# Two row blocks of attention joined behind the experts, with the last chunk settled inside, and a shorter lag

## The chip, the cores and the metric

One NeuronCore of a Trainium2 chip runs the whole program. The metric is the device time of one execution in microseconds. The median of three runs of the kernel before is 915.72 us.

## The reference

Input: `x` (64, 64, 64, 4) and `txt` (64, 32, 64), float32; 64 batches, T = 96 tokens (64 made from `x`, 32 from `txt`), width 64.

```
h = concat(mean over hidden of (x @ W^T + b), txt)      # (64, 96, 64)
h = h + state_space_layers(layernorm(h))                # four layers
h = h + moe(layernorm(h))                               # 16 experts, top 2, then a layernorm
h = h + attention(layernorm(h))                         # 8 heads of width 64
h = h + recurrence(layernorm(h))                        # 96 steps over the tokens

attention: q, k, v = x Wq + bq, ...;  scores = q k^T / 8
           position i sees j < i only; row 0 is all zero;  out = softmax(scores) v Wu + bu
recurrence: i, g, o from xt U + b + h V;  c' = h c + i g;  h' = o tanh(c')
```

Since a token sees only earlier ones, attention can be done in blocks of 32 rows (tokens), each of which needs only the tokens up to its end, and the recurrence can run as soon as the row block of its step is done.

## The kernel before

All work is one program over five engines that hand over by semaphores. What follows the state-space layers is a sequence of NSLOT = 152 slots (the loops `for g in range(NSLOT)` of GpSimd, ScalarE, VectorE and TensorE). NPR = 96 of them are expert slots: in each, TensorE does one pair of experts for 512 tokens, `up` (L1491, 4 matmuls) and `down` (L1478) of two slots ago, VectorE weighs the input (`weigh`, L1004), ScalarE applies the relu (L684, or L686 and L688 in halves). Eight slots finish a quarter-chunk product that ScalarE copies out (`product_out`, L675). Sixteen slots finish a chunk of 16 tokens; there are NC = 6 chunks, two to a row block.

A finished chunk is *settled* in parts at slots given by SB and LATER (LAST for the last chunk): `sums_out` turns the sums through PSUM bank 7 (L1393), VectorE adds them (`settle` 0 to 3), centres them, GpSimd squares them (L547), takes the power -1/2 (L550), multiplies (L553) and applies gamma (L557), twice (second time for the attention's norm), `norm_out` turns the result (L1400), and two copies on ScalarE (`turned`, L670) and two on VectorE (parts 13, 14, L996) put it where attention reads it. `borrow` makes TensorE wait until the last reader has freed bank 7.

AT names the slots after which the slot loop stops and a row block of attention is done: 47, 79 and 107. Row block 0 has 4 units, block 1 has 8, block 2 has 16; a unit is (row block, group of 16 batches, share of the group), and a group makes one unit in block 0, two in block 1, four in block 2. (The prediction calls them the first, second and third attention, or row blocks 1, 2 and 3 as the change's title does.) For a group TensorE makes *queries* in two halves into banks 6 and 7 (L1504); ScalarE copies bank 6 (`u_out`, L694) and VectorE bank 7 (L1015). For a unit: scores (L1518, or L1525 with the mask L1528); in block 0 the mask is added by VectorE (L1048) and the scores are turned (`turn_s`, L1536); VectorE takes the maximum (L1054) and subtracts it (L1058); ScalarE exponentiates (L715); VectorE sums (L1036) and inverts (L1039 to L1043); GpSimd multiplies (L581); TensorE turns the probabilities (`turn_p`, L1546) and the keys (`turn_keys`, L1556); ScalarE copies the first (L729), VectorE the second (L1066); `gather` (L1574) multiplies them, its results are copied by both engines (L706, L1027); `project` (L1585) closes a group and ScalarE copies the output with the bias (L720).

Inside an attention all engines walk x over the units and a tail. In round x the unit x is scored, x - 2 is turned, x - 3 gathered, x - 4 projected (DRAIN = 4). On ScalarE, the exponential of unit x comes first in the round, then the copies of the next group's queries; `next_u` says in which round a group's two query halves are made. Attention starts only when all four engines have finished their slots, and TensorE waits for all of its copies before it goes on.

The recurrence: step t runs in slot LS0 + t = 56 + t (`step_at`): TensorE `gates_h` (L1454, 12 matmuls of 32 columns), ScalarE tanh of the gates (L743; from step 52 on L745 and L747), VectorE L1107 and L1113, ScalarE L751, VectorE L1120 and L1122; every four steps `gates_x` makes the next inputs (L1440) and `out_tp` turns outputs (L1469). So 24 steps share slots 56 to 79 with experts, 16 share 80 to 95, 12 run in 96 to 107 beside the last chunk's settling, and 44 run alone. Before the steps of a chunk, the attention output of that chunk must be turned (`att_out`, L1409), added, normalised and copied (`att_residual`, `norm`, `normed`, `turn_x`, `copy_x`, L737): the parts of XLATER at the slots of XB.

## Time and profile before

| | us |
|---|---|
| median of 3 runs | 915.72 |
| lowest and highest | 906.75, 916.69 |
| the profiled execution | 910.88 |
| its span | 909.2 |
| TensorE, VectorE, ScalarE, GpSimd busy | 714.3, 556.1, 344.6, 251.5 |
| mean granted TensorE clock | 0.827 of full |

All stretches below are cut from this one execution; the time of an execution is its span and 1.7 us around it. A busy share over the whole span says little here, because stages with different limits follow one another.

### The profile page before, as it was taken

The numbers are of one execution on the slowest core, as the hardware profiler recorded it, in microseconds if no ns is written. First come the engines' busy times: TensorE is split into PE (matmuls) and PEld (weight loads), VectorE is DVE, ScalarE is ACT, GpSimd is POOL, SyncE is SP. The second block draws the span as 40 slices with busy tenths as digits, with TensorE's granted clock in tenths as the row PEclk, the third lists the DMA queues.
The fourth block names the chain that finished last, engine by engine and source line by source line (L and its number), as shares of the span: only waits on it lengthen the run. The fifth ranks groups of instructions, "written<-read, shape, count | busy, mean of one in ns | idle before, by whom it ended". The sixth has DMA issues, their size and how long they took to land.

```text
span 909.2 us, 16503 instructions
## 1 busy us (share of the span) xinstructions
PE 714.3 (79%) x6414; PEld 420.1 (46%) x6414; DVE 556.1 (61%) x1128; ACT 344.6 (38%) x656; POOL 251.5 (28%) x223
## 2 busy tenths in 40 slices
PE   4686888654799998567899987978985599976675
PEld 3673656344322222254234435654434377755554
DVE  4848557769566563552685757657846477746543
ACT  2232343424244554123435543354442244432332
POOL 3338567547000330100240212212313032311100
PEclk9998887965599999668999998899975599985555
DMA  9730000000253341000222200002200000000000
GB/s 189 122 70 4 2 1 1 1 1 0 82 168 115 107 141 32 1 1 1 93 76 77 94 36 1 1 9 75 59 4 7 6 2 1 2 1 6 8 9 13
DMA packets 42403, 36.86 MB, mean 41 GB/s; under 512 B 20888, under 2 KB 29848, under 8 KB 42328
## 3 DMA queue, kind: packets, MB, share of 16 engines
q1 hardware_dynamic: 41242, 35.57, 14.9%
q8 instruction: 52, 0.85, 0.4%
q10 hardware_dynamic: 1088, 0.26, 0.2%
q14 instruction: 21, 0.17, 0.1%
HBM read 33.85 MB, written 1.97 MB: 39 GB/s over the span
## 4 chain that ended last, share of the span: by engine, by line
PE 51%; DVE 28%; ACT 8%; issue 6%; POOL 2%; DMA 2%; SPq 1%; POOLq 0%; DVEq 0%; ACTq 0%
PE PS L1491 9%; PE PS L1478 9%; PE PS L1454 4%; PE PS L1504 3%; PE PS L1525 3%; PE PS L1574 3%; PE PS L1585 2%; DVE XC L863 2%; PE PS L1546 2%; DVE am L1054 2%; DVE LS L1113 2%; DVE st L845 2%; DMA BIG<-in_x 2%; PE PS L1556 2%; ACT Y L639 2%
## 5 line engine op out<-in xcount | busy, mean ns | idle before, releaser
L1491 PE MATMUL PS<-Y,W1f 64*128 64x512 f32 x384 | 114.4, 675 | 4.5 <-DVE Y L1004 2.9
L1478 PE MATMUL PS<-XC,w2s 128*64 128x512 f32 x384 | 106.4, 635 | 0.8 <-ACT XC L688 0.5
L1454 PE MATMUL PS<-LS,V 64*64 64x32 f32 x1140 | 68.4, 264 | 45.1 <-DVE LS L1120 44.9
L1454 PEld LDWEIGHTS PS<-LS,V 64*64 64x64 f32 x1140 | 56.5, 181 | 76.4 <-DVE LS L1120 68.9
L684 ACT ACTIVATE XC<-PS 128x1024 f32<-128x1024 f32 x61 | 62.3, 1021 | 55.7 <-PE PS L1478 44.7
L1004 DVE TENSOR_TENSOR Y<-XD,UF 128x512 f32<-128x512 f32 x96 | 69.5, 735 | 16.9 <-DMA UF<-gd 9.1
L1107 DVE SCALAR_TENSOR_TENSOR LS<-LS 128x32 f32<-128x32 f32 x96 | 22.6, 236 | 62.1 <-ACT LS L743 32.5
L547 POOL TENSOR_TENSOR Y<-XC 128x512 f32<-128x512 f32 x12 | 13.6, 1135 | 161.7 <-DVE XC L984 161.7
L1478 PEld LDWEIGHTS PS<-XC,w2s 128*64 128x64 f32 x384 | 19.6, 138 | 77.2 <-issue 59.9
L1491 PEld LDWEIGHTS PS<-Y,W1f 64*128 64x128 f32 x384 | 30.6, 193 | 45.8 <-issue 23.1
L1504 PE MATMUL PS<-BIG,MMs 64*128 64x512 f32 x96 | 36.6, 845 | 17.3 <-ACT UT L694 6.9
L178 POOL TENSOR_TENSOR st<-st,mhalf 128x8 f32<-128x8 f32 x24 | 39.3, 1637 | 37.6 <-DVE st L848 37.6
L751 ACT ACTIVATE LS<-LS 128x32 f32<-128x32 f32 x96 | 22.0, 229 | 59.3 <-DVE LS L1113 58.5
L1054 DVE TENSOR_REDUCE am<-PS 128x8 f32<-128x768 f32 (+2 forms) x28 | 29.5, 1053 | 21.1 <-PE PS L1528 16.2
L581 POOL TENSOR_TENSOR Y<-Y,am 128x768 f32<-128x768 f32 (+1 forms) x10 | 16.4, 1643 | 92.3 <-DVE am L1043 52.5
L1264 PE MATMUL PS<-ident,UT 128*128 128x128 f32 x120 | 24.2, 337 | 21.4 <-POOL UT L180 21.4
L1120 DVE SCALAR_TENSOR_TENSOR LS<-LS 128x32 f32<-128x32 f32 x96 | 22.3, 232 | 30.0 <-ACT LS L751 30.0
L1574 PE MATMUL PS<-Y,UT 32*64 32x128 f32 (+2 forms) x768 | 36.2, 281 | 5.5 <-DVE EX L1027 2.8
L1440 PE MATMUL PS<-XD,U 65*64 65x128 f32 x288 | 33.7, 359 | 3.7 <-ACT XD L720 3.7
L1251 PE MATMUL PS<-bdt,UF 128*128 128x128 f32 x192 | 29.4, 300 | 6.8 <-ACT Y L634 6.8
L743 ACT ACTIVATE LS<-PS 128x96 f32<-128x96 f32 x52 | 13.0, 250 | 56.0 <-PE PS L1454 54.3
L562 POOL TENSOR_TENSOR bdt<-bds 128x512 f32<-128x512 f32 x6 | 7.4, 1235 | 96.1 <-DVE bds L1091 96.1
(238 smaller groups left out, 1508.0 us busy)
## 6 DMA issues: line engine op xcount, KB each, us to landing
UF<-gd SPq DMA_DIRECT2D x192, 128.0 KB, 2.9
BIG<-in_x SPq DMA_DIRECT2D x8, 512.0 KB, 12.2
out<-X SPq DMA_DIRECT2D x48, 32.0 KB, 2.0
W1f<-in_L_ffn_w SPq DMA_DIRECT2D x2, 512.0 KB, 6.0
EX<-in_L_ffn_w SPq DMA_DIRECT2D x1, 1024.0 KB, 16.3
H<-in_txt SPq DMA_DIRECT2D x2, 256.0 KB, 12.4
w2s<-in_L_ffn_w SPq DMA_DIRECT2D x1, 512.0 KB, 10.7
gd<-EX SPq DMA_DIRECT2D x6, 64.0 KB, 1.7
```

The source lines that it names most:

```text
L178: pool.tensor_tensor(st[:, 3, sj], st[:, 2, sj], mhalf[:, 0:KC * 2], ALU.pow).then_inc(S("s_r"), 1)
L684: act.activation(Hb[:, b:b + 2, :], PS[:, b:b + 2, :], ACT.Relu).then_inc(S("m_h"), 1)
L1004: dve.tensor_tensor(Rb[:, n % 4, :], XD[:, q * 512:(q + 1) * 512], GB[:, n % NS, :], ALU.mult).then_inc(S("m_x"), 1)
L1054: dve.tensor_reduce(stat_a(x, 0), scores(UNITS[x]), AX_X, ALU.max).then_inc(S("a_mx"), 1)
L1251: mm = pe.matmul(PS[:, j % 3, k * 128:k * 128 + 128], UF[:, j * KC + k, :], bdt[:, l + 1, :], start=(k == 0), stop=False)
L1440: mm = pe.matmul(dst[64 * h:64 * h + 64], U3[:, g, :], xt[:, :, h, :], start=first, stop=(k == 0), skip_group_check=True)
L1454: mm = pe.matmul(PS[r, b, o:o + HN], V3[r, g, :], HB[r, (t - 1) % 4, :], start=False, stop=True, skip_group_check=True)
L1478: mm = pe.matmul(PS[64 * h:64 * h + 64, 6, :], w2s[:, 2 * p + h, :], Hb[:, n % 2 * 2 + h, :], start=(p == 0), stop=(p == E // 2 - 1))
L1491: mm = pe.matmul(PS[:, n % 2 * 2 + h, :], W1f[r, 2 * p + h, :], Rb[r, n % 4, :], start=True, stop=True)
L1504: pe.matmul(PS[:, 6 + h, :], MMs[p, half, :, :].rearrange("p a d -> p (a d)"), XAb[p, b0:b0 + GA, RB * r:RB * r + RB], start=True, stop=Tr ...
L1525: pe.matmul(PS[:, a, b * w:(b + 1) * w], Ub[G % 2][p, b0 % GA + b, :, :].rearrange("p h i -> p (h i)"), XAb[p, b0 + b, 0:w], start=(b == 0 ...
L1574: mm = pe.matmul(PS[64 * a:64 * a + 64, 4 + (JOBS[u] + k) % 2, x * 128:(x + 1) * 128], XT[p, u % 2, x, :], PT[p, u % 2, a, x, :], start=Tr ...
```

## The change

It has five parts. (1) The stops are AT = (47, 95): row block 0 after slot 47 as before, and row blocks 1 and 2 as one attention of 24 units behind the last expert slot. (2) The last chunk is no longer settled in slots of its own: VectorE's parts, GpSimd's parts and TensorE's three turnings are put into the first seven rounds of that attention (TAIL_DVE, TAIL_POOL, and x - us[0] in 0, 1, 6). (3) XS = T // 3 = 32 steps of the recurrence run in slots 56 to 87, none in 88 to 95, and the other 64 from slot LS1 = 104 on; the residual parts of chunks 2 to 5 start at slots 96, 106, 120 and 136. NSLOT becomes 168. (4) The lags are a table by row block: in blocks 0 and 1 a unit is turned and gathered one round after its scores and projected two after; block 2 keeps 2, 3, 4. (5) ScalarE copies both banks of queries with one instruction of 128x1024 and VectorE none; on ScalarE the projection's copy, the query copies and the copy of the turned probabilities stand ahead of the exponential (except the second query half of blocks 1 and 2, which stands behind it).

```diff
-        DRAIN = 4
+        LAGS = ((1, 1, 2), (1, 1, 2), (2, 3, 4))
+
+        def due(x, us, k):
+            return [u for u in us if u + LAGS[UNITS[u][0]][k] == x and (k < 2 or UNITS[u][6])]
+
+        TAIL_DVE = {0: (0, 1), 1: (2, 3, 4, 5), 2: (6, 7), 3: (8, 9), 4: (10,), 5: (11, 12), 6: (13, 14)}
+        TAIL_POOL = {0: ("sq0",), 1: ("pw0", "mu0", "ga"), 3: ("sq1",), 4: ("pw1", "mu1")}
...
-        NT = 12
-        AT = (3 * E - 1, 5 * E - 1, NPR + NT - 1)
+        AT = (3 * E - 1, NPR - 1)
         LS0 = 3 * E + 8
-        XS = AT[2] + 1 - LS0
-        NSLOT = LS0 + T
+        XS = T // 3
+        LS1 = NPR + 8
+        NSLOT = LS1 + T - XS
...
-        XB = (3 * E, 3 * E + 8, 5 * E, 5 * E + 8, NPR + NT, NPR + NT + 9)
+        XB = (3 * E, 3 * E + 8, NPR, NPR + 10, NPR + 24, NPR + 40)
...
         def step_at(g):
-            return g - LS0 if 0 <= g - LS0 < T else None
+            return g - LS0 if LS0 <= g < LS0 + XS else g - LS1 + XS if g >= LS1 else None
...
-            return ((0, 1), (v,), ((), (0,), (1,), ())[v] if r == 2 else ())[r]
+            return ((0, 1), (0, 1) if r == 1 and (v == 0) == (UNITS[first_unit(G + 1)][0] == 1) else (), ((), (0,), (1,), ())[v] if r == 2 else ())[r]
...
                     pool.tensor_tensor(probs(u), probs(u), spread_a(u, 3), ALU.mult).then_inc(S("a_pn"), 1)
+                    for part in TAIL_POOL.get(u - us[0], ()) if UNITS[u][0] else ():
+                        settle(NC - 1, part)
...
             def u_out(G, half):
-                act.wait_ge(S("a_u"), 4 * G + 2 * half + 1)
+                act.wait_ge(S("a_u"), 2 * G + half + 1)
                 if G >= 2:
                     act.wait_ge(S("a_s"), first_unit(G - 1))
-                act.activation(Ub[G % 2][:, :, 2 * half, :], PS[:, 6, :].rearrange("p (b i) -> p b i", i=RB), ACT.Copy).then_inc(S("u_ev0"), 1)
+                act.activation(Ub[G % 2][:, :, 2 * half:2 * half + 2, :].rearrange("p b h i -> p h b i"),
+                               PS[:, 6:8, :].rearrange("p h (b i) -> p h b i", i=RB), ACT.Copy).then_inc(S("u_ev0"), 1)
...
-                    if x in us:
-                        act.wait_ge(S("a_sub"), x + 1)
-                        act.activation(probs(x), probs(x), ACT.Exp).then_inc(S("a_e"), 1)
...
-                    if x in us and 0 in next_u(x, us):
+                    if 0 in nxt:
                         u_out(UNITS[x][1] + 1, 0)
-                    if x - 2 in us:
-                        u, W = x - 2, rows(UNITS[x - 2])
+                    if 1 in nxt and r == 0:
+                        u_out(UNITS[x][1] + 1, 1)
+                    for u in due(x, us, 0):
+                        W = rows(UNITS[u])
                         act.wait_ge(S("a_t"), u + 1)
...
                         act.activation(PT[0:W, u % 2, :, :, :], PS[0:W, 2:4, :].rearrange("p a (x c) -> p a x c", x=4), ACT.Copy).then_inc(S("pt_ev"), 1)
-                    if x - 3 in us:
-                        z_out(x - 3)
-                    if x in us and 1 in next_u(x, us):
+                    if x in us:
+                        act.wait_ge(S("a_sub"), x + 1)
+                        act.activation(probs(x), probs(x), ACT.Exp).then_inc(S("a_e"), 1)
+                    if 1 in nxt and r:
                         u_out(UNITS[x][1] + 1, 1)
+                    for u in due(x, us, 1):
+                        z_out(u)
+                    if UNITS[us[0]][0] and x == us[0] + 6:
+                        turned(NC - 1, 0)
+                        turned(NC - 1, 1)
...
-            def u_out(G, half):
-                dve.wait_ge(S("a_u"), 4 * G + 2 * half + 2)
...
-                    if x - 3 in us:
-                        z_out(x - 3)
-                    if x in us and 1 in next_u(x, us):
-                        u_out(UNITS[x][1] + 1, 1)
-
+                    for u in due(x, us, 1):
+                        z_out(u)
+                    for k in TAIL_DVE.get(x - us[0], ()) if UNITS[us[0]][0] else ():
+                        settle(NC - 1, k)
...
-                for x in range(us[0], us[-1] + DRAIN + 2):
+                for x in range(us[0], us[-1] + LAGS[-1][2] + 1):
+                    r, nxt = (UNITS[x][0], next_u(x, us)) if x in us else (None, ())
                     if x in us:
                         score(x)
-                    if x - 4 in us and UNITS[x - 4][6]:
-                        project(UNITS[x - 4][1], x - 4, nU)
+                    for u in due(x, us, 2):
+                        project(UNITS[u][1], u, nU)
                         nO += 1
-                    if x in us and 0 in next_u(x, us):
+                    if 0 in nxt:
                         queries(UNITS[x][1] + 1, 0, nU, nO, nX)
                         nU += 1
-                    if x in us and UNITS[x][0] == 0:
+                    if r == 0:
                         turn_s(x)
-                    if x - 2 in us:
-                        turn_p(x - 2)
-                        turn_keys(x - 2, nU)
+                        if 1 in nxt:
+                            queries(UNITS[x][1] + 1, 1, nU, nO, nX)
+                            nU += 1
+                    for u in due(x, us, 0):
+                        turn_p(u)
+                        turn_keys(u, nU)
                         nX += 1
-                    if x - 3 in us:
-                        gather(x - 3)
-                    if x in us and 1 in next_u(x, us):
+                    if r == 1 and 1 in nxt:
                         queries(UNITS[x][1] + 1, 1, nU, nO, nX)
                         nU += 1
+                    for u in due(x, us, 1):
+                        gather(u)
+                    if r == 2 and 1 in nxt:
+                        queries(UNITS[x][1] + 1, 1, nU, nO, nX)
+                        nU += 1
+                    if UNITS[us[0]][0] and x - us[0] in (0, 1, 6):
+                        pe.wait_ge(S("u_ev0"), nU)
+                        pe.wait_ge(S("xt_ev"), nX)
+                        if x - us[0] < 2:
+                            sums_out(NC - 1, x - us[0])
+                        else:
+                            norm_out(NC - 1)
+                        borrow()
...
-                if t is not None and t % 4 >= 2 and 4 * (t // 4 + 1) < T and LS0 + 4 * (t // 4) + 3 not in AT:
+                if t is not None and t % 4 >= 2 and 4 * (t // 4 + 1) < T and step_at(g + 4 - t % 4) is not None:
                     gates_x(t // 4 + 1, (0, 1) if t % 4 == 2 else (2,))
-                if g == LS0 - 1:
-                    gates_x(0, (0, 1, 2))
+                if t is None and step_at(g + 1) is not None:
+                    gates_x(step_at(g + 1) // 4, (0, 1, 2))
```

## Rows read from the trace of the kernel before

**Rows 1.** Windows by stage: stretch, each engine busy (instructions), clock, DMA.
```profile
355.26:438.73 83.47, 56.36 (x769) 32.08 (x769) 35.85 (x47) 21.51 (x28) 7.64 (x4) 0.73 0.03 9
438.73:537.52 98.79, 93.65 (x748) 37.97 (x749) 71.06 (x181) 49.77 (x111) 26.51 (x20) 0.97 0.25 80
537.52:614.83 77.31, 61.14 (x784) 42.26 (x785) 45.58 (x58) 28.60 (x36) 15.21 (x8) 0.91 0.03 7
614.83:677.87 63.04, 57.13 (x464) 25.48 (x464) 43.87 (x116) 26.63 (x67) 17.09 (x13) 0.89 0.15 46
677.87:711.54 33.67, 16.35 (x243) 12.28 (x241) 20.41 (x65) 9.26 (x29) 8.75 (x7) 0.57 0.03 7
711.54:810.30 98.76, 88.00 (x865) 65.01 (x865) 63.69 (x96) 40.95 (x52) 23.50 (x16) 0.91 0.01 2
810.30:909.20 98.90, 66.90 (x860) 50.55 (x860) 49.32 (x207) 29.20 (x134) 7.48 (x6) 0.51 0.04 9
```

**Rows 2.** Timeline of the first attention: start, us, engine, line, operation [idle before].
```profile
359.31 1.15 PE L1518 MATMUL PS<-UT,BIG 64*32 64x128 f32 x64 [0.88 <-DVE UT L1015]
...
360.39 1.13 PE L1504 MATMUL PS<-BIG,MMs 64*128 64x512 f32 x4
...
362.92 1.22 DVE L1054 TENSOR_REDUCE am<-PS 128x32 f32<-128x1024 f32 x1 [0.59 <-PE PS L1536]
...
365.44 1.06 ACT L715 ACTIVATE Y<-Y 128x1024 f32<-128x1024 f32 x1 [6.41 <-DVE Y L1058]
...
367.03 2.08 PE L1504 MATMUL PS<-BIG,MMs 64*128 64x512 f32 x4 [4.15 <-ACT EX L694]
...
371.74 1.91 POOL L581 TENSOR_TENSOR Y<-Y,am 128x1024 f32<-128x1024 f32 x1 [28.46 <-DVE am L1041]
...
412.69 1.13 PE L1546 MATMUL PS<-ident,BIG 128*128 128x128 f32 x8
...
414.33 1.10 PE L1574 MATMUL PS<-Y,UT 32*64 32x128 f32 x32
...
418.60 1.94 PE L1585 MATMUL PS<-EX,NPt 128*64 128x512 f32 x8 [1.13 <-DVE EX L1027]
...
420.57 1.16 ACT L720 ACTIVATE XD<-PS,bus 128x512 f32<-128x512 f32 x1 [2.48 <-PE PS L1585]
```

**Rows 3.** Expert slots: window of L1491 alone; tanh in slots 63 and 79.
```profile
270.00:350.00 80.00, 39.17 (x140) 10.23 (x136) 1.00 0.38 113
...
485.87 0.25 ACT L743 ACTIVATE LS<-PS 128x96 f32<-128x96 f32 x1 [1.09 <-PE PS L1454]
...
533.18 0.25 ACT L743 ACTIVATE LS<-PS 128x96 f32<-128x96 f32 x1
```

**Rows 4.** Timeline of the second attention, two units' scores.
```profile
541.51 2.00 PE L1525 MATMUL PS<-BIG,UT 64*128 64x64 f32 x32 [0.84 <-ACT UT L694]
...
552.98 3.68 PE L1525 MATMUL PS<-BIG,EX 64*128 64x64 f32 x32 [3.09 <-ACT EX L694]
```

**Rows 5.** Timeline of slots 96 to 107, settling beside steps.
```profile
695.09 1.04 POOL L547 TENSOR_TENSOR Y<-XC 128x512 f32<-128x512 f32 x1 [4.74 <-DVE XC L984]
...
695.14 1.03 DVE L1113 SCALAR_TENSOR_TENSOR LS<-LS 128x32 f32<-128x32 f32 x1
...
699.91 1.64 POOL L550 TENSOR_TENSOR st<-st,mhalf 128x8 f32<-128x8 f32 x1 [3.78 <-DVE st L991]
```

**Rows 6.** Timeline of the third attention, keys turned behind a query copy.
```profile
745.97 0.89 PE L1556 MATMUL PS<-ident,BIG 64*96 64x64 f32 x8 [0.95 <-DVE UT L1015]
```

**Rows 7.** Timeline of the last stretch, ScalarE.
```profile
811.57 0.22 ACT L745 ACTIVATE LS<-PS 128x64 f32<-128x64 f32 x1 [1.95 <-PE PS L1454]
...
826.18 0.59 ACT L737 ACTIVATE XD<-PS 64x512 f32<-64x512 f32 x1 [0.67 <-PE PS L1416]
...
863.22 0.22 ACT L745 ACTIVATE LS<-PS 128x64 f32<-128x64 f32 x1 [0.96 <-PE PS L1454]
...
903.50 0.22 ACT L745 ACTIVATE LS<-PS 128x64 f32<-128x64 f32 x1 [0.97 <-PE PS L1454]
```

42 lines of the change are left out of this document (14 added, 28 removed).

## The prediction

> **What bounds the kernel now.** I read the stages first [rows 1], because the change only moves work between stages and no stage has one limit throughout. The seven stretches are: first attention (row block 1, 4 units), expert slots 48 to 79, second attention (row block 2, 8 units), expert slots 80 to 95, slots 96 to 107 (recurrence steps 40 to 51 beside the settling of the last chunk), third attention (row block 3, 16 units), and the 44 remaining steps. They sum to 553.9 us of the 909.2; what lies before 355.26 is untouched. The reader is to see three kinds. In the expert slots TensorE is busy 91 to 95% and bounds. In the third attention it is busy 89% and bounds too. In the first attention it is busy 56 of 83 us at a mean clock of 0.73: it waits, and falls to its lower level (1.2 GHz) while it waits. In slots 96 to 107 and in the last stretch it is busy half to two thirds at 0.51 to 0.57, and the chain of one step decides. Second I read the order of the first attention [rows 2]: ScalarE's copy of the next queries stands behind the exponential, which waits for the subtraction, so TensorE idles 4.15 us before the second half of the queries and then does them in 2.08 instead of 1.13 us. That was the case in each of the three units that have a successor.
>
> **The first attention.** By [rows 2] I walk the units with the new order, at full clock. Queries 1.13 and one wide copy 1.06 (the nearest row of that width is the exponential), twice: 4.5. Unit 0: scores 1.15, mask addition 1.22, turning of the scores 1.1, maximum 1.22, subtraction 1.22, with 0.1 at each hand-over: 6.4. After it each unit has scores, queries, scores turned, queries, probabilities turned 1.1, keys 0.65, gathering 1.1 twice with a copy of 0.6 between, and its probabilities wait for the sum (1.2), the reciprocal (0.6) and GpSimd's product 1.91. I get 11.9 for unit 1, 13.1 for unit 2 (the projection of 1.94 and its copy of 1.16 now stand ahead of the queries, on the path), 11.7 for unit 3, and 13.3 for the drain, in which one unit is left instead of three. Sum 60.9. The idles in it are mostly under 2 us, so I allow a low spell or two, 5 us: **66 instead of 83.5**, a gain of 17. Its bounds: 61 with no low spell, and 83, where each unit keeps today's cycle and the shorter drain is lost again in low clock.
>
> **Slots 48 to 95 in one piece.** Before 79, nothing changes. Slots 80 to 87 keep steps 24 to 31, at the rate of slots 63 to 79: 47.3 us over 16 intervals, 2.96 each [rows 3]. The residual work of chunks 2 and 3 is no longer there. Slots 88 to 95 have no step; plain slots go at 80.00 / 35 = 2.29 us (140 matmuls, four a slot) [rows 3]. So 98.8 + 23.7 + 18.3 - 0.9 (no outputs to turn at slot 79, one stop and restart less) = 140, against 98.8 + 63.0. Bounds 137 and 144.
>
> **The joint attention.** Queries and copies 4.5. In row block 2 a group has two units. From [rows 2, 4]: the scores take 2.33 with their mask; in a unit with queries the path is scores 2.35, the sum ahead of the maximum on VectorE, product until 4.25, turned 1.1, keys 0.6, copy of the keys 0.4, second queries 1.13, gathering 1.1: 8.65; in the other 7.55. Group 16.2, of which TensorE works 14.6. Four: 65. Turning one unit behind means that the turning of a unit waits for GpSimd's product within the same round; what fills the wait are queries and projection.
>
> The settling inside it [rows 5]. Three times TensorE hands out the eighth bank and waits in place until it is free, with the next scores queued behind. In round 0 it waits for the second copy of the queries, turns, and waits for two additions: 3.1 us. In round 1 about 1.8. In round 6 two copies on ScalarE and two on VectorE, about 1.05 each: 4.2. GpSimd has power 1.64, product 1.04 and gamma 1.3 queued ahead of the product for unit 2 of the attention: 2.6 us that the turning waits; again 1.3 for the second power. VectorE has settling ahead of the next sum in rounds 0, 2 and 4: 2.7. Sum 15.7. The lower bound is 10.7, what slots 96 to 107 take today over twelve bare steps of 1.918 [rows 1, 7]; the upper is 22, if each of the seven rounds waits 3.1.
>
> Row block 3 keeps its lags. Of its 98.8 us, 6 are the two cold queries at the start, which go. Three times [rows 6] TensorE waits 0.95 for VectorE's copy of the queries, which stands behind a subtraction; the copy is now ahead of the exponential on ScalarE: -2.8. The last unit of row block 2 is turned, gathered and projected among the first scores: +5.4, less 2.5 for scores that are no longer cold. 98.8 - 6.0 - 2.8 + 2.9 = 93.
>
> A wait of 3.09 us ahead of the third unit's scores already brought the low clock today, and 32 matmuls took 3.68 instead of 2.00 [rows 4]. In the new order I see three waits of over 3 us (behind GpSimd's three settling products, before and after the second norm), each worth 2: +6. Sum 4.5 + 65 + 15.7 + 93 + 6 = **184**, against 77.3 + 98.8 + 33.7 for the three stretches that it replaces. Bounds 173 and 200.
>
> The Trainium skill, SBUF - State Buffer, section "SBUF: two separate sides", speaks against this placement: VectorE and GpSimd share a pair of ports under an exclusive lock, and a VectorE operation with two SBUF inputs waits out a GpSimd operation. The trace agrees: a multiply-add of only 128x32 took 1.03 us, from 695.14 to 696.17, beside GpSimd's square that ran from 695.09 to 696.13 [rows 5]. By that rule the two additions of settling that read SBUF twice could each wait 1.91 behind a product, some 4 us more; by my walk they fall between products, and I add nothing.
>
> **After the attention.** No step can start: chunk 2's attention output must be turned, added, normalised, turned and copied, and nothing lies beside it. By its parts: three turnings 0.7 to 1.1, four additions 0.42, two reductions and a centring 0.7 each, GpSimd 1.09, 1.64 and 1.14, two copies 0.6, twelve gate matmuls and the first tanh: 14.7 us to the first tanh. The same chain for chunk 4, beside steps, had its copy at 826.18 after 810.3 [rows 7], 16 us later, so 14 to 17. Then 63 intervals of 1.918 (863.22 to 903.50, 21 steps) = 120.8. Chunks 4 and 5 cost (863.22 - 811.57) - 22 x 1.918 = 9.4, or 4.7 each; there are three now: 14.2. The end, 5.7, stays. **155.4 against 98.9**. Bounds 152 and 159.
>
> **Sum.** 355.3 + 66 + 140 + 184 + 155.4 = 900.7 us of span, 902.4 with the 1.7 around it (910.88 was the profiled execution's time for a span of 909.2). That is 0.991 of its own time. The median of the runs shown is 915.72, 0.5% above that execution; on its scale the forecast is 907. The gain by parts: -17.5 first attention, -21.8 expert slots, -25.8 joint attention with settling, +56.5 at the end. So nearly all of what merging gives is paid back by 20 steps and one chunk that lose their cover.
>
> **Rivals.** *The first attention keeps its cycle.* Today's 12.75 us a unit are near my 11.7 to 13.1, because gathering now stands between a unit's scores and the next. If copies ahead of exponentials change nothing there but the drain, the stage is 75, and the whole 909.7: no difference. For: TensorE's own work is 42 us at full clock and over 70 at the low one [rows 1, 2]. Against: the 4.15 us waits are gone by the order itself.
>
> *The waits cost little.* If the clock stays high and settling costs its lower bound (10.7, no low spells), the joint attention is 173 and the first 61: 884.7. For: the clock was 0.91 in both later attentions [rows 1]. Against: GpSimd's queue is in order.
>
> *The other side: the lag of one puts TensorE at 1.2 GHz.* Place: row block 2's units. A group has 14.6 us of matmuls, which at the low level are 29 against a cycle of 16.2, +13. If two of four groups run low, +26, less the 6 counted, and 7 more in the first attention: 927.7, slower than before. It decides from about one and a half low groups on. For: a wait of 3.09 was enough once [rows 4]. Against: queries and projection fill most waits. The Trainium skill, TensorE: Matmul & The Clock Gate, section "What's actually happening", says that the slow state is the default and activity releases it; here the clock did return within the first attention: queries took 2.08 at 367.03, gathering 1.10 at 414.33 [rows 2], the levels of 1.2 and 2.4 GHz. The price above needs neither.
>
> *A delayed start only:* chunk 2's chain at 17 and steps that do not reach 1.918: +4, inside the range.
>
> **How the numbers follow.** Forecast 0.37, first attention unchanged 0.27, cheap waits 0.20, low clock 0.12, rest 0.04. On the median's scale they lie at 907, 916, 891 and 934. The range takes in the first three and stops short of the last: 888 to 924; the forecast's own is 899 to 914. About 1% is what a measurement of this kernel can tell from no change, the runs shown spread by that. The forecast lies at -0.9%, so a bit under half of it counts as faster: 0.37 x 0.47 + 0.27 x 0.15 + 0.20 + 0.02 = 0.44; slower is the low clock and a tail, 0.15; the rest, 0.41, is the same.
>
> **What would show it.** Right: a first attention of 62 to 70 us with no idle over 2.5 us ahead of queries; the joint one starting near 561 (355.3 + 66 + 140) and lasting 176 to 192; three waits on the eighth bank in its first seven rounds; 13 to 17 us without a step behind it; 64 steps at 1.9. Wrong: a first attention over 75 or a joint one outside 173 to 200, slots 80 to 95 over 46 us, or a step interval other than 1.9.

## The result, and the profile after

The kernel became slower: 923.75 us (median of 20 runs, 913.73 to 927.47) against 911.35 us for the kernel before, run on the same chip (20 runs, 906.67 to 917.17), a ratio of the means of 1.0109 with an interval of 1.0077 to 1.0141. The forecast was 907 with a range of 888 to 924: the time lies just inside the upper end, but the kernel moved the other way. The 20 times fall into two groups, nine from 913.7 to 919.4 at granted clocks of 0.812 to 0.816 and eleven from 923.2 to 927.5 at 0.793 to 0.804, and the profiled execution, with a span of 924.8 us and a mean clock of 0.797, is one of the upper group.

The windows of the changed kernel by stage, with the columns of [rows 1]: first attention, expert slots 48 to 95, the joint attention up to row block 3's first scores, the rest of it, and what follows.

```profile
355.62:424.58 68.96, 51.15 (x768) 28.89 (x769) 30.33 (x39) 25.61 (x28) 7.65 (x4) 0.80 0.04 11
424.58:563.47 138.89, 133.53 (x1021) 52.05 (x1021) 96.31 (x243) 72.64 (x154) 36.75 (x27) 0.98 0.25 79
563.47:669.12 105.65, 81.89 (x741) 55.25 (x741) 44.52 (x58) 34.04 (x37) 21.94 (x14) 0.66 0.00 1
669.12:768.18 99.06, 91.01 (x921) 68.26 (x921) 62.18 (x93) 47.09 (x54) 25.43 (x17) 0.90 0.01 1
768.18:924.80 156.62, 102.53 (x1280) 77.22 (x1280) 78.98 (x313) 43.30 (x196) 14.88 (x12) 0.51 0.04 8
```

| stage | forecast | after | before [rows 1] |
|---|---|---|---|
| first attention | 66 | 69.0 | 83.5 |
| expert slots 48 to 95 | 140 | 138.9 | 98.8 + 63.0 |
| joint attention with settling | 184 (91 + 93) | 204.7 (105.65 + 99.1) | 77.3 + 98.8 + 33.7 |
| behind it | 155.4 | 156.6 | 98.9 |

Three of the four stages came within 3 us. The whole miss is the joint attention, and most of it is its first part, row block 2, called "the part" below: from the first queries (563.47) to row block 3's first scores (669.12). Its granted clock is 0.66. A window at 0.66 whose clock has only two levels is at the lower one (1.2 GHz) for about two thirds of its time. The timeline of the changed kernel in that part shows where it falls (start, duration, engine, line, operation, idle time before it and what ended it):

```profile
572.74 2.08 PE L1505 MATMUL PS<-BIG,MMs 64*128 64x512 f32 x4
...
581.23 3.68 PE L1526 MATMUL PS<-BIG,UT 64*128 64x64 f32 x32 [0.97 <-DVE Y L982]
...
605.81 1.64 POOL L556 TENSOR_TENSOR st<-st,mhalf 128x8 f32<-128x8 f32 x1 [8.23 <-DVE st L1006]
607.52 1.04 POOL L559 TENSOR_TENSOR Y<-XC,st 128x512 f32<-128x512 f32 x1
608.64 1.27 POOL L563 TENSOR_TENSOR Y<-Y,gam 128x512 f32<-128x512 f32 x1
609.87 1.90 POOL L587 TENSOR_TENSOR Y<-Y,am 128x1024 f32<-128x1024 f32 x1
...
611.83 1.97 PE L1547 MATMUL PS<-ident,Y 128*128 128x128 f32 x8 [3.56 <-POOL Y L587]
613.73 1.12 PE L1557 MATMUL PS<-ident,BIG 64*64 64x64 f32 x16
615.42 1.98 PE L1575 MATMUL PS<-Y,UT 64*64 64x128 f32 x32 [0.57 <-ACT Y L738]
617.34 3.68 PE L1526 MATMUL PS<-BIG,UT 64*128 64x64 f32 x32
...
642.91 1.97 PE L1547 MATMUL PS<-ident,Y 128*128 128x128 f32 x8 [4.07 <-POOL Y L587]
...
652.78 3.68 PE L1526 MATMUL PS<-BIG,EX 64*128 64x64 f32 x32 [3.25 <-issue]
```

The first two lines are of the opening: queries at 2.08 instead of 1.13 and scores at 3.68 instead of 2.00, so the part is at the low clock almost from its start. Then the reader is to see a chain of three lines at 605.81: GpSimd does settling's power, product and gamma, 3.95 us, ahead of the attention's product (L587). The turning of the probabilities (L1547) stands right behind that product, since with lag one it belongs to the same round, so TensorE waits 3.56 us; 2.7 of them are GpSimd's three operations, for VectorE had the reciprocal that the product needs ready at 607.13. Then turning takes 1.97 instead of 1.10 us, gathering 1.98 instead of 1.10, scores 3.68 instead of 2.00: the lower of the two clock levels, until the queries at 621.49 are done (2.08), some 12 us. The wait alone is not the price; the wait and what runs slowly behind it are.

The other forecasts hold in rows. In the first attention of the changed kernel the second half of the queries, which waited 4.15 us and took 2.08 in [rows 2], now follows the turned scores at once (366.13), because ScalarE's copy of the first half (365.05) stands ahead of the exponential (368.58):

```profile
364.93 1.09 PE L1537 MATMUL PS<-ident,Y 128*128 128x128 f32 x8
365.05 1.03 ACT L702 ACTIVATE EX<-PS 128x1024 f32<-128x1024 f32 x1 [3.99 <-PE PS L1505]
...
366.13 1.13 PE L1505 MATMUL PS<-BIG,MMs 64*128 64x512 f32 x4
...
368.58 1.06 ACT L741 ACTIVATE Y<-Y 128x1024 f32<-128x1024 f32 x1 [0.25 <-DVE Y L1063]
```

And behind the joint attention the chain of chunk 2 lies bare: its output is turned, GpSimd's product ends it, and the first tanh comes at 782.67, 14.5 us after 768.18 (forecast 14.7).

```profile
768.18 0.63 PE L1411 MATMUL PS<-ident,XD 128*128 128x128 f32 x4 [1.43 <-ACT XD L727]
...
777.94 1.11 PE L1418 MATMUL PS<-ident,Y 128*128 128x128 f32 x4 [7.37 <-POOL Y L576]
...
782.67 0.22 ACT L760 ACTIVATE LS<-PS 128x64 f32<-128x64 f32 x1 [2.99 <-PE PS L1456]
```

### The profile page after: what moved, and what is told of

Same layout as the page of the kernel before. It is cut to its first block, busy times and chain, and to the rows that moved or that the text cites. A ratio compares the mean times of both kernels' runs of the same rounds, so it can differ in the third digit from the quotient of the medians.

```text
span 924.8 us, 16444 instructions
## 1 busy us (share of the span) xinstructions
PE 736.7 (80%) x6414; PEld 437.7 (47%) x6414; DVE 537.7 (58%) x1104; ACT 361.3 (39%) x667; POOL 252.1 (27%) x223
## 3 DMA queue, kind: packets, MB, share of 16 engines
HBM read 33.85 MB, written 1.97 MB: 39 GB/s over the span
## 4 chain that ended last, share of the span: by engine, by line
PE 58%; DVE 20%; ACT 7%; issue 6%; POOL 4%; DMA 2%; SPq 1%; POOLq 0%; DVEq 0%; ACTq 0%
PE PS L1493 10%; PE PS L1480 9%; PE PS L1456 5%; PE PS L1575 4%; PE PS L1526 4%; PE PS L1505 4%; PE PS L1547 3%; PE PS L1586 3%; DVE XC L878 2%; PE PS L1442 2%; PE PS L1244 2%; PE PS L1557 2%; PE PS L1253 2%; DMA BIG<-in_x 2%; DVE st L860 1%
## 5 line engine op out<-in xcount | busy, mean ns | idle before, releaser
L1493 PE MATMUL PS<-Y,W1f 64*128 64x512 f32 x384 | 111.4, 660 | 4.7 <-DVE Y L1019 3.2
L1456 PE MATMUL PS<-LS,V 64*64 64x32 f32 x1140 | 71.3, 271 | 38.2 <-DVE LS L1122 38.0
L1456 PEld LDWEIGHTS PS<-LS,V 64*64 64x64 f32 x1140 | 59.2, 189 | 71.4 <-DVE LS L1122 63.8
L692 ACT ACTIVATE XC<-PS 128x1024 f32<-128x1024 f32 x68 | 69.5, 1022 | 59.6 <-PE PS L1480 48.9
L1019 DVE TENSOR_TENSOR Y<-XD,UF 128x512 f32<-128x512 f32 x96 | 70.2, 744 | 17.2 <-DMA UF<-gd 9.4
L1575 PE MATMUL PS<-Y,UT 32*64 32x128 f32 (+2 forms) x768 | 40.9, 317 | 9.9 <-ACT Y L738 4.1
L738 ACT ACTIVATE Y<-PS 96x1024 f32<-96x1024 f32 (+1 forms) x28 | 28.6, 1022 | 44.9 <-PE PS L1547 44.9
L1575 PEld LDWEIGHTS PS<-Y,UT 32*64 32x64 f32 (+2 forms) x768 | 32.7, 158 | 15.3 <-ACT Y L738 7.5
L760 ACT ACTIVATE LS<-PS 128x64 f32<-128x64 f32 x64 | 14.3, 224 | 64.9 <-PE PS L1456 64.9
L1442 PE MATMUL PS<-XD,U 65*64 65x128 f32 x288 | 36.6, 382 | 1.5 <-ACT XD L752 1.5
L587 POOL TENSOR_TENSOR P<-P,am 128x768 f32<-128x768 f32 (+1 forms) x9 | 15.0, 1663 | 80.6 <-DVE am L1050 71.1
```

Source lines behind the costliest of these rows:

```text
L692: act.activation(Hb[:, b:b + 2, :], PS[:, b:b + 2, :], ACT.Relu).then_inc(S("m_h"), 1)
L738: act.activation(PT[0:W, u % 2, :, :, :], PS[0:W, 2:4, :].rearrange("p a (x c) -> p a x c", x=4), ACT.Copy).then_inc(S("pt_ev"), 1)
L1019: dve.tensor_tensor(Rb[:, n % 4, :], XD[:, q * 512:(q + 1) * 512], GB[:, n % NS, :], ALU.mult).then_inc(S("m_x"), 1)
L1442: mm = pe.matmul(dst[64 * h:64 * h + 64], U3[:, g, :], xt[:, :, h, :], start=first, stop=(k == 0), skip_group_check=True)
L1456: mm = pe.matmul(PS[r, b, o:o + HN], V3[r, g, :], HB[r, (t - 1) % 4, :], start=False, stop=True, skip_group_check=True)
L1493: mm = pe.matmul(PS[:, n % 2 * 2 + h, :], W1f[r, 2 * p + h, :], Rb[r, n % 4, :], start=True, stop=True)
```

## The experiments

My theory after the result: lag one in row block 2 makes TensorE wait within the round for what stands in other engines' queues, and each such wait brings the low clock. Rivals: settling inside the attention is dear by itself; merging is; a ring over the engines holds the pace down. All runs are measured against the kernel before on the same chip. "Whole" is from the joint attention's first queries to the end of its last projection. These are the forms of the merged kernel:

| form | part | clock in it | whole | median | ratio to before |
|---|---|---|---|---|---|
| as changed | 105.65 | 0.66 | 203.3 | 923.8 | 1.0109 |
| m_lag2 | 78.2 | 0.78 | 170.6 | 892.3 | 0.9798 |
| m_settle_out | 80.2 | 0.80 | 177.5 | 921.9 | 1.0111 |
| m_out_lag2 | 67.9 | 0.79 | 160.3 | 903.9 | 0.9891 |
| m_fill | 100.6 | 0.78 | 199.4 | 920.8 | 1.0128 |
| m_expfirst | 105.6 | 0.69 | 203.0 | 923.7 | 1.0127 |
| m_defer | 98.4 | 0.72 | 195.5 | 917.0 | 1.0104 |
| m_lend | 99.6 | 0.69 | 195.6 | 919.7 | 1.0151 |
| m_lend_defer | 96.1 | 0.70 | 190.7 | 915.8 | 1.0078 |
| m_three | 89.2 | 0.73 | 185.2 | 908.1 | 0.9950 |
| m_lag2_lend | 72.5 | 0.81 | 164.9 | 889.0 | 0.9798 |
| m_lag2_three | 78.6 | 0.76 | 171.1 | 895.5 | 0.9836 |

The medians of different calls differ by chip and hour: that of the kernel before was 905.9 to 911.4, so ratios compare kernels and the windows compare mechanisms. Every window is of one execution. The first attention, whose code is the same in all these forms, took from 63.8 (m_lend_defer) to 68.0 us (m_settle_out) from its first queries to the end of its last projection, so a difference of under some 4 us between two windows shows nothing. The windows of the changed kernel, from an execution 3 us over its median, have a second trace beside them: m_expfirst, whose change did nothing, has the same waits (3.56, 4.08 and 3.25 us) and a part of 105.6.

**Lag two in row block 2** (m_lag2)

```diff
-        LAGS = ((1, 1, 2), (1, 1, 2), (2, 3, 4))
+        LAGS = ((1, 1, 2), (2, 3, 4), (2, 3, 4))
```

> The changed kernel with row block 2 back at lags 2, 3, 4; everything else as changed. Lag theory (turning one unit behind makes TensorE wait for GpSimd's product in every round of row block 2, and it then works at its lower clock level): the stretch from the first queries of the joint attention to row block 3's first scores falls from 105.7 us to 80 to 90, the joint attention from 204.7 to 180 to 190, the kernel to about 0.99 of before. Settling theory (the last chunk's settling inside the attention is what costs): that stretch stays over 98 us and the kernel stays at 1.01 of before.

Measured: ratio 0.9798 (0.9748 to 0.9848); the part 78.2 us, and what follows it 93.6 at a clock of 1.00, a little better than the 80 to 90 of the lag theory. This one constant turns a slower kernel into one faster than before. Its windows, with the columns of [rows 1]:

```profile
559.21:637.40 78.19, 60.98 (x644) 41.05 (x645) 42.25 (x55) 30.52 (x33) 21.93 (x14) 0.78 0.00 1
637.40:731.00 93.60, 88.59 (x1016) 66.57 (x1016) 63.61 (x96) 50.08 (x58) 25.40 (x17) 1.00 0.01 2
```

VectorE, ScalarE and GpSimd do the same work in the part as above (42, 31, 22 us). TensorE has 97 matmuls less there, since one turning, two gatherings and a projection slide behind it (5.9 us at full clock), and they are done in the second window, which is nevertheless 5.5 us shorter. The rest of the difference can be read from the same two windows. TensorE is idle for 17.2 us of this part (78.19 - 60.98) and for 23.8 of the changed kernel's (105.65 - 81.89), 6.6 more. It is busy 20.9 us longer there, of which 5.9 are the work that slid; the other 15.0 are the same matmuls done more slowly. So the low clock costs more than twice what the waits themselves do.

**Matmuls into the wait** (m_fill)

```diff
             def turn_p(u):
...
-                pe.wait_ge(S("a_pn"), u + 1)
...
                     pe.wait_ge(S("pt_ev"), u)
+                if UNITS[u][0] == 1:
+                    for x in range(8):
+                        pe.transpose(PS[:, 2 + x // 4, x % 4 * 128:(x % 4 + 1) * 128], ident[:, :], ident[:, :])
+                pe.wait_ge(S("a_pn"), u + 1)
```

> The changed kernel with eight extra 128x128 transposes of the identity in each unit of row block 2, ahead of TensorE's wait for GpSimd's product, into the banks that the turning writes next (results unchanged). Clock theory (the waits are short, and what costs is the low level that follows them): the granted clock of the stretch rises from 0.65 to over 0.8 and the stretch falls from 105.7 to 90 to 97 us although it has 8 x 1.1 us more work. Wait theory (the chain product, turning, copy, gathering is itself the cost, at any clock): the clock may rise, but the stretch stays within 3 us of 105.7 or grows by up to 9.

Measured: ratio 1.0128 (1.0066 to 1.0189), the part 100.6 us, clock 0.78 in it; neither theory's numbers. Eight more transposes a unit, whose results are overwritten, go with a clock that is 0.12 higher. The part is 5 us shorter, hardly more than two windows of the same code can differ, and the kernel as a whole is not faster by its ratio. What the trace shows beyond that is in the shares: 56 of the transposes lie in the part and take 9.3 us there, and TensorE is busy 79.0 us with them, so its own work takes 69.7 instead of 81.9, while its idle time falls only from 23.8 to 21.7. m_lag2 has the same mean clock and is 22.4 us shorter; 5.9 of these are the work that slid, 9.3 the transposes, 4.4 idle time and 2.8 slower matmuls.

**Settling taken out** (m_settle_out: the last chunk is settled as in the kernel before, in twelve slots of its own behind slot 95, here without steps beside it; lag one stays)

```diff
+        NT = 12
-        AT = (3 * E - 1, NPR - 1)
+        AT = (3 * E - 1, NPR + NT - 1)
...
-                    for k in TAIL_DVE.get(x - us[0], ()) if UNITS[us[0]][0] else ():
-                        settle(NC - 1, k)
```

> The changed kernel, but the last chunk is settled in 12 slots of its own ahead of the joint attention, with no step beside it; lags as changed. Settling theory: the stretch of row block 2 falls from 105.7 to 80 or less. Lag theory: it falls by the waits on the eighth bank and GpSimd's queue, 8 to 16 us, and stays over 88. In both the 12 slots add 18 to 26 us ahead of it, so the kernel is 5 to 15 us slower than the changed one by the lag theory and equal to it by the settling theory.

Measured: ratio 1.0111 (1.0056 to 1.0166), the part 80.2 us, as the settling theory said, and the twelve slots ahead of it take back nearly all of that (the joint attention starts at 586.25 instead of 563.47). The part is far shorter with lag one kept, so lag one alone does not explain it; nor does settling, which stays in m_lag2. Its timeline also settles a term of the sum, by the scores of units 2, 4 and 6, counted from 0: the distance from unit 2 to unit 4 and from 4 to 6 is 16.4 us, and the forecast for a group of two units with lag one was 16.2.

```profile
610.24 2.00 PE L1523 MATMUL PS<-BIG,EX 64*128 64x64 f32 x32
...
626.63 2.00 PE L1523 MATMUL PS<-BIG,UT 64*128 64x64 f32 x32
...
643.02 2.00 PE L1523 MATMUL PS<-BIG,EX 64*128 64x64 f32 x32
```

**The fourth corner** (m_out_lag2: settling out and lag two)

> The merged attention with the last chunk settled in twelve slots behind it (no settling inside), and row block 2 turned two units behind, gathered three behind. With lag one the part from the first queries to row block 3's first scores took 105.7 us with settling and 80.2 without; with lag two it took 78.2 with settling. Theory A (settling's waits are dear only with lag one, since they throw TensorE to 1.2 GHz and the lag-one order cannot get out): settling costs about 10 us here, so the part takes 66 to 70 and the kernel is 12 to 20 us faster than the lag-one form of it (921.9), 902 to 910. Theory B (lag and settling are two prices that add, 27 for the one and 25 for the other): the part takes 50 to 56. Theory C (settling costs nothing with lag two): 76 to 80, the kernel 915 to 920.

The edit is that of m_settle_out with that of m_lag2; the twelve slots stand ahead of the joint attention, which starts at 583.82, and not behind it as the expectation has it.

Measured: ratio 0.9891 (0.9851 to 0.9932), the part 67.9 us. So theory A, within its numbers. Over the whole of the joint attention settling costs 10.3 us with lag two (170.6 - 160.3) and 25.8 with lag one (203.3 - 177.5); lag one costs 17.2 without settling and 32.7 with it. Together they cost 15.5 more than apart. The four corners again, by what TensorE does in the part:

| form | part | busy | idle |
|---|---|---|---|
| lag one, settling inside (as changed) | 105.65 | 81.9 | 23.8 |
| lag one, settling out | 80.2 | 67.0 | 13.2 |
| lag two, settling inside | 78.2 | 61.0 | 17.2 |
| lag two, settling out | 67.9 | 57.6 | 10.3 |

Beyond the 5.9 us that slide with lag two, lag one adds 3.5 us of busy and 2.9 of idle time without settling, and 15.0 and 6.6 with it. Three quarters of what the two cost beyond their sum is slower matmuls.

The size of that extra is less sure than its sign. The forms without settling start their attention cold (queries of 2.08 behind a wait of 3.46 us), m_lag2 does not (1.13), which by the time from the first queries to the first mask (10.0 and 6.5 us; 8.7 as changed) makes settling 3.6 us dearer with lag two and 1.3 with lag one: 13.9 and 27.1. And by the ratios of whole kernels lag one costs 3.1% with settling inside and 2.2% without (2.2% also between u_112_112 and u_112_234 below). The difference of 0.9%, 8 us, is as large as the four intervals together leave open. At full clock the group takes 14.6 us with lag two, from 620.82 to 635.42, so 1.8 of 16.4 are lag one's own:

```profile
620.82 2.00 PE L1523 MATMUL PS<-BIG,UT 64*128 64x64 f32 x32 [0.31 <-DVE P L1062]
...
635.42 2.00 PE L1523 MATMUL PS<-BIG,EX 64*128 64x64 f32 x32
```

**The stages as before, lag one in both or only in row block 1** (u_112_112, u_112_234). Both keep the order of the stages of the kernel before and take the new attention code; the first has the lags 1, 1, 2 in row blocks 1 and 2, the second 2, 3, 4 in row block 2.

> Only the attention code of the change (lags 1, 1, 2 in row blocks 1 and 2, wide query copies ahead of exponentials), with the slot plan of before: three attentions, last chunk settled in slots 96 to 107 beside steps. The first attention takes 69 us as in the changed kernel (83.5 before). Lag theory: the second attention takes 85 to 95 us where it took 77.3, so that the kernel gains only some 3 us on before, within 1%. Settling theory: the second attention takes 70 to 77, and the kernel is 0.975 to 0.985 of before.

> The order of the stages as before (row blocks 2 and 3 apart, twelve slots with steps 40 to 51 and the last chunk's settling between), with the new copies, lag one in row block 1 only, lags two and three in row block 2. The form with lag one in both measured 0.9953 of before with a second attention of 91.8 us, against 77.3 before. Theory A (lag one is what costs row block 2, merging by itself gains little): second attention 73 to 78, first 68, kernel 888 to 895, 0.975 to 0.983 of before, about the same as the merged kernel with lag two (892.3). Theory B (merging is worth some 10 us by itself): kernel 900 to 905.

Measured: ratios 0.9953 (0.9923 to 0.9982) and 0.9736 (0.9650 to 0.9822). The second attention takes 89.6 us, from 516.69 to 606.31, with lag one and 80.9, from 518.32 to 599.24, with lag two; 77.3 before. (The traced execution of u_112_112, 897.3 us, is the fastest of ten with a median of 905.8.) My 73 to 78 for the latter was a miss. Its clock there is 0.79, but a cold start alone is not shown to be the cause: in u_234_234 the same stage with the same code starts colder still (queries of 2.08 at 535.12) and takes 76.1 us from the first queries to the end of the last projection, against 79.1 here. The kernels' medians, 893.8 here and 892.3 for the merged m_lag2, cannot be told apart, nor can their ratios: merging by itself gives nothing that is measured.

**The copies ahead of exponentials alone** (u_234_234: stages and lags as before)

> The order of the stages as before and all lags as before; only the query copies (one wide copy on ScalarE, ahead of the exponential) are new. It parts the 15 us that the first attention gained. If the copies alone give it, the first attention takes 68 to 71 and the kernel is within 3 us of the form with lag one in row block 1. If the lag of one gives it (a shorter drain, the third unit behind no longer waiting), the first attention takes 76 to 82 and the kernel is 8 to 14 us slower than that form. I expect something between: 72 to 76.

Measured: 0.9878 (0.9812 to 0.9944). The first attention takes 77.1 us, from 354.90 to 432.01, against 83.5 before and 65.3, from 352.72 to 418.03, in u_112_234, which adds lag one. So the copies give some 6 and lag one with its shorter drain 8 to 12, for the same attention took 69.0 in the changed kernel. With the copies goes TensorE's order: the second half of the queries now stands ahead of the turning of probabilities, in this run too. My 72 to 76 was too good for them.

**Exponential ahead of the copy of turned probabilities** (m_expfirst)

```diff
+                    early = r == 1
+                    if early:
+                        act.wait_ge(S("a_sub"), x + 1)
+                        act.activation(probs(x), probs(x), ACT.Exp).then_inc(S("a_e"), 1)
                     for u in due(x, us, 0):
...
-                    if x in us:
+                    if x in us and not early:
```

> The changed kernel, lag one and settling inside, but ScalarE does a unit's exponential of row block 2 ahead of the copy of the unit before's turned probabilities. Theory A (with lag one the exponential behind that copy closes a ring over ScalarE, VectorE, GpSimd and TensorE; at 1.2 GHz the ring is longer than the cycle and holds TensorE down): the part up to row block 3's first scores takes 84 to 95 instead of 105.7, the kernel 903 to 913. Theory B (the ring over the product alone, turning waits within the round for GpSimd, and the waits of settling do it): 101 to 108, the kernel within 4 us of the changed one (923.8).

Measured: 1.0127 (1.0097 to 1.0158), the part 105.6 us. The ring through ScalarE falls; this was my theory and it was wrong.

**One place in GpSimd's queue, and the wait for the eighth bank behind the scores** (m_defer, m_lend, and both in m_lend_defer)

```diff
-        TAIL_POOL = {0: ("sq0",), 1: ("pw0", "mu0", "ga"), 3: ("sq1",), 4: ("pw1", "mu1")}
+        TAIL_POOL = {0: ("sq0",), 2: ("pw0", "mu0", "ga"), 3: ("sq1",), 5: ("pw1", "mu1")}
```

```diff
                     if x in us:
                         score(x)
+                    if UNITS[us[0]][0] and x - us[0] in (1, 2, 7):
+                        borrow()
...
                             norm_out(NC - 1)
-                        borrow()
```

> The changed kernel (lag one, settling inside) with GpSimd's settling products one place later in its queue: power, product and gamma of the first norm behind the attention's product of the third unit instead of ahead of it, power and product of the second norm behind that of the sixth. In the changed kernel the turning waited 3.56 us at 611.83 and 4.07 at 642.91 for those products, and what followed ran at 1.2 GHz (turning 1.97, keys 1.12, gathering 1.99, scores 3.68). Theory A (each such wait costs itself and the low clock behind it): 2.7 of the first wait and 1.4 of the second go, and 4 to 5 us of low clock behind the first; the part up to row block 3's first scores takes 95 to 100 instead of 105.7, the kernel 913 to 918. Theory B (only the waits count): 101 to 103, the kernel 919 to 921. Theory C (the place in GpSimd's queue does not matter): 104 to 106, the kernel 924.

> The changed kernel, but TensorE does the next unit's scores between handing out the eighth bank and waiting until it is free (the scores do not use it). The three waits in place (0.98, 0.98 and 3.25 us in the changed kernel) then have 2.0 to 3.7 us of scores beside them. Theory A (waits in place and the low clock behind them): the part takes 96 to 101 instead of 105.7, the kernel 914 to 919. Theory B (the low clock comes from GpSimd's product alone): 102 to 105, the kernel within 4 us of 923.8.

> Both: the later place in GpSimd's queue and the scores ahead of the wait for the eighth bank, lag one kept. Theory A (lag one costs nothing that settling's waits do not bring, since without settling the unit cycle was 8.8 and 7.6 us as forecast): the part takes 84 to 92, near the 80.2 that it took without settling, the kernel 902 to 911. Theory B (lag one beside any settling stays at 1.2 GHz): over 95, the kernel over 913.

Measured: ratios 1.0104 (1.0032 to 1.0176), 1.0151 (1.0099 to 1.0202) and 1.0078 (1.0043 to 1.0113); the part 98.4, 99.6 and 96.1 us. Each alone does what was expected in the part, by 7 and 6 us in one execution each, but by its ratio none of the three can be told from the changed kernel's 1.0109. Both together take 9.6 off the part, where 14 to 22 were expected: theory B's number. The timeline of m_lend_defer shows what took their place:

```profile
607.23 1.09 PE L1547 MATMUL PS<-ident,Y 128*128 128x128 f32 x8 [0.90 <-POOL Y L587]
...
611.30 0.68 DVE L989 TENSOR_TENSOR H<-H,Y 128x512 f32<-128x512 f32 x1
612.02 0.69 DVE L996 TENSOR_REDUCE st<-H 128x8 f32<-128x512 f32 x1
...
612.62 1.21 DVE L1043 TENSOR_REDUCE am<-P 128x16 f32<-128x1024 f32 x1
...
614.20 1.90 POOL L587 TENSOR_TENSOR P<-P,am 128x1024 f32<-128x1024 f32 x1 [2.95 <-DVE am L1050]
...
616.16 1.97 PE L1547 MATMUL PS<-ident,P 128*128 128x128 f32 x8 [2.23 <-POOL P L587]
...
623.78 3.68 PE L1526 MATMUL PS<-BIG,UT 64*128 64x64 f32 x32
```

Unit 2's turning (607.23) now waits 0.90 instead of 3.56 and runs fast. For unit 3 VectorE has settling's addition and reduction, 1.4 us, ahead of the sum over the exponentials (L1043). Sum, product and turning are one chain, so the wait becomes 2.23, and 1.2 GHz follows it through the next scores.

**VectorE's settling in its idle time** (m_three: as the last, and VectorE's parts 6 to 12 ahead of the copy of the turned keys instead of at the end of the round)

```diff
-        TAIL_DVE = {0: (0, 1), 1: (2, 3, 4, 5), 2: (6, 7), 3: (8, 9), 4: (10,), 5: (11, 12), 6: (13, 14)}
-        TAIL_POOL = {0: ("sq0",), 1: ("pw0", "mu0", "ga"), 3: ("sq1",), 4: ("pw1", "mu1")}
+        TAIL_DVE = {0: (0, 1), 1: (2, 3, 4, 5), 6: (13, 14)}
+        EARLY_DVE = {2: (6, 7), 4: (8, 9), 5: (10,), 6: (11, 12)}
+        TAIL_POOL = {0: ("sq0",), 2: ("pw0", "mu0", "ga"), 4: ("sq1",), 5: ("pw1", "mu1")}
```

> The kernel with both cures and lag one (96.1 us in the part, kernel 915.8), and VectorE's settling of rounds 2 to 6 moved from ahead of the next sum over exponentials to ahead of the copy of the turned keys, where VectorE was idle for 1.3 to 1.5 us (the second norm slides one round on, GpSimd's square with it). Theory A (what is left is VectorE's 1.4 us ahead of the sum: the turning's wait grows from 0.9 to 2.2 us and brings 1.2 GHz): the part takes 84 to 90, the kernel 904 to 910. Theory B (lag one beside settling stays low whatever the order): 94 to 98, the kernel within 4 us of 915.8.

Measured: ratio 0.9950 (0.9909 to 0.9992), median 908.1, the part 89.2 us: theory A, and against theory B, whose number m_lend_defer had given. The same turning of unit 3 waits 0.91 and takes 1.09, and the scores of unit 4 follow those of unit 3 after 7.6 us, as without settling:

```profile
603.81 2.00 PE L1529 MATMUL PS<-BIG,EX 64*128 64x64 f32 x32
...
611.43 2.00 PE L1529 MATMUL PS<-BIG,UT 64*128 64x64 f32 x32
...
615.73 1.09 PE L1550 MATMUL PS<-ident,P 128*128 128x128 f32 x8 [0.91 <-POOL P L588]
```

Lag one with settling inside is thus brought from 105.65 to 89.2 by places in three queues, with nothing removed. It is not free of low clock: TensorE is still busy 75.5 us in the part, against 67.0 without settling, and settling's own turnings are only 2 of the difference.

**The two best places with lag two** (m_lag2_lend, m_lag2_three)

> The merged kernel with lags two and three in row block 2 (892.3 us, 78.2 us in the part) and the scores ahead of the wait for the eighth bank. It waited 0.98, 2.51 and 3.61 us there, each time ahead of scores of 3.68 instead of 2.00 us. Theory A: 4 to 5 of these 7.1 us and some 3 us of low clock go; the part takes 69 to 73, the kernel 884 to 888. Rival (a wait moves on to the next queries, which use the bank): 76 to 78, the kernel 890 to 893.

> The same places with lags two and three in row block 2 (with the late wait alone: 72.5 us in the part, kernel 889.0). The turning takes the product of two rounds ago, so neither GpSimd's nor VectorE's place should matter much: theory A says 70 to 74, the kernel 886 to 891; if the places matter as much as with lag one, 62 to 67 and 878 to 883.

Measured: 0.9798 (0.9742 to 0.9854) with a part of 72.5 us and 0.9836 (0.9749 to 0.9922) with one of 78.6. The late wait for the bank takes 5.7 us off the part, as expected; the kernel's 889.0 is a little above the 884 to 888, and by its ratio it can't be told from m_lag2. Moving VectorE's parts as well gives them back, which neither number of the expectation foresaw. A round with lag two is shorter, and the second norm slid one round too far: its turning (L1405 of m_lag2_three) waits for GpSimd, and the scores behind it run slow.

```profile
619.03 1.09 PE L1405 MATMUL PS<-ident,Y 128*128 128x128 f32 x4 [3.94 <-POOL Y L560]
620.04 3.68 PE L1529 MATMUL PS<-BIG,EX 64*128 64x64 f32 x32
```

So m_lag2, m_lag2_lend and u_112_234 beat both kernels, by 2.0 to 2.6% against the one before.

## Why the prediction was wrong

The stages outside the joint attention were right by their own steps. First attention: 69.0 for 66; against before, the order of copies gives some 6 and the lag with its drain 8 to 12. (I had said that the wait of 4.15 us came in each of three units; it was 4.15, 4.15 and 2.47.) Expert slots: 138.9 for 140. The end: 14.5 us bare chain for 14.7, 136.4 us of steps, from 782.67 to 919.1, for 135. That merging is about paid back by the steps that lose their cover is confirmed by m_lag2 against u_112_234.

The step that failed: "In the new order I see three waits of over 3 us (behind GpSimd's three settling products, before and after the second norm), each worth 2: +6. Sum 4.5 + 65 + 15.7 + 93 + 6 = **184**". That put the joint attention at 184 with bounds of 173 and 200, and a time outside these was named as a sign of being wrong; it took 204.7. The three places were right, and the waits are there at 611.83 (3.56), 642.91 (4.07) and 652.78 (3.25). The price of the low clock was wrong. At the durations that the rows have at full clock (scores 2.00 with a mask of 0.39, turning 1.09, keys 0.68, gathering 1.10, queries 1.13, projection 1.94, settling's turnings 0.65) the matmuls of the part come to 58 us, and TensorE is busy 82. So the low clock costs some 24 us there, by this estimate, where the sum has 6; without it the part would have taken 82 us, and the sum has 85 (4.5 + 65 + 15.7). I missed it in three ways.

- *The price of a low spell.* I took 2 us each, from one spell with 32 slow matmuls [rows 4]. In the changed kernel the spell behind 611.83 alone has 0.87 on the turning, 0.44 on the keys, 0.88 on the gathering, 1.68 on the scores, 0.2 on the mask and 0.95 on the queries: 5.0. With lag one the round's other operations stand behind the wait, and they were slow until the next turning, which took 1.41.
- *The waits that I did not count as such.* I had the queries and their copies at the start, and VectorE's 1.4 us ahead of the sum, as costs of their own size and at full clock. Units 0 to 2 run their scores at 3.68, before the first wait that I had priced. In m_lend_defer a wait of 2.23 us was enough.
- *Settling and lag one as terms that add.* Settling was 15.7 in the sum. By the windows it costs 10.3 with lag two, near my lower bound of 10.7 (13.9 if the start is set equal), and 25.8 with lag one, over the upper one of 22. The 65 for four groups were right only at full clock (16.4 measured for 16.2): with settling out, the opening and the four groups, 69.5 in the sum, took 80.2, with the low clock in the first group and the last.

The rest of the joint attention, 99.1 for 93, is the lag once more: the last unit of row block 2 waits for GpSimd's product within the round, and is turned, gathered and projected at low clock among the first scores. Settling has no share in it: m_settle_out has the same wait (2.80 at 670.61) and takes 97.3 us to the end of the last projection, against 97.6. With lag two the stretch took 93.6. In the timeline of the changed kernel:

```profile
673.27 1.97 PE L1547 MATMUL PS<-ident,BIG 128*128 128x128 f32 x8 [2.80 <-POOL BIG L587]
...
681.06 3.68 PE L1586 MATMUL PS<-EX,NPt 128*64 128x512 f32 x8
```

What happened is the rival "the lag of one puts TensorE at 1.2 GHz", to which I gave 0.12. Its span of 927.7, for two low groups of four, was 3 us off, in part by luck: it had 7 us of low clock in the first attention, which came out 3 over the forecast, and none in row block 3's stretch, which came out 6 over. My reason against it, that queries and projection fill most waits, held in m_settle_out for the middle of the part alone. The rows had enough for more: one wait of 3.09 had brought the low clock already [rows 4], and my own walk put three such waits among eight units.

Still open: how large the extra cost of settling beside lag one is (15 us by the windows, 8 by the ratios), and what parts the two groups of times of the changed kernel, of which only the upper was traced. m_three is 9 us above the part without settling. The first queries' waits for the wide copies (1.16 and 1.12 in the changed kernel) and the start that is at times warm (2.00 at 569.58 in m_lend_defer) and at times cold (3.68 at 568.59 in the changed kernel) were not tried apart.

## What to carry to other kernels

When a software pipeline is made one stage shorter, list for each wait that now falls within the round everything that stands ahead of it in the releasing engine's queue, and follow it back through every engine of the chain (here sum on VectorE, product on GpSimd, turning on TensorE). Then price each such wait at its own length plus the slow work behind it; here a wait of 3.56 us was followed by another 5.0. Foreign work put in between, as the settling here, cost more beside a lag that waits within the round (25.8 us in the windows) than beside one that does not (10.3), and most of the excess was slow matmuls and not waiting. Shares of busy and idle time in one stage tell the two apart.

## What the runs showed of the hardware

A wait of TensorE of 0.90 us (607.23 in m_lend_defer) was followed by turning at 1.09 us; one of 2.23 us nine microseconds later by turning at 1.97, queries at 2.08 and scores at 3.68, and the clock was back only in the midst of the projection at 627.92. I had expected it only of waits over 3 us. The length of one wait does not decide it alone. In m_three a wait of 0.91 (615.73) left turning at 1.09, but the queries at 618.14, behind another of 0.71, took 2.08, and the next scores 2.00 again. In m_lend_defer a wait of 2.80 (665.28) left turning at 1.10, and only the gathering behind it took 1.99. Short waits close together did it too: at the start of the joint attention of the changed kernel TensorE waited 0.74, 1.16 and 1.12 us, with 1.1 to 1.7 us of queries between, and the scores at 568.59 took 3.68. In m_lag2 the same waits left the first scores at 2.00 and the queries behind them at 2.08. And work that does nothing went with a higher clock: with 56 more transposes in it the part had 0.78 instead of 0.66, and TensorE's other work took 12 us less.
